# The prologue of a four-layer conditional kernel: batch weights from a small product, loads and first products in another order

## The chip, the cores and the metric

The kernel runs on one core of one Trainium2 chip. The metric is the device time of one execution in microseconds (us); lower is better. PE is TensorE, DVE is VectorE, ACT is ScalarE, POOL is GpSimd, SP is SyncE.

## The reference, cut to what matters

`x` has 16 batches of 128 rows by 128 channels, and `cond_8` has 8 weights for each batch. Four layers are added to `x` one after the other:

```
x = x + L0(x)   # the expert with the largest weight of the batch: silu gated MLP, 128 -> 256 -> 128, biases
x = x + L1(x)   # out = x W_base^T + b_base, and the low-rank part:
                #   h = einsum('btc,erc->bter', x, As)
                #   lora = einsum('bter,eor,be->bto', h, Bs, cond_8);  out + 2 * lora
x = x + L2(x)   # w_bot = einsum('bg,got->bot', cond_8, weight * mask);  x w_bot^T + bias
x = x + L3(x)   # softmax of cond_8, best two of 8 experts, gated gelu MLP 128 -> 512 -> 128,
                #   weighted sum, and one shared MLP of the same shape for all batches
```

## The kernel before

`x` is kept transposed in SBUF, channels on the partitions and 16 times 128 rows on the free axis. Every engine runs its own list of instructions, written out by hand, and the lists meet at semaphores. No planner moves anything: the order in the code is the order on the engine.

**The prologue (lines 257 to 526).** SP loads `cond_sb` (the weights and small tables, 16 partitions), `lora_sb` (the factors of L1) and `w2_sb` (the weights of L2). ACT's queue loads `cond_rep` (the batch weights, repeated on all 128 partitions by the DMA's access pattern), `small_sb` and all of `x`. While PE waits for inputs it multiplies constants into a bank that nobody reads (`warm`, line 487: five products of 512 columns, then some of 128). DVE finds the best experts of each batch (lines 684 to 689); a small product on PE (line 506) turns the expert numbers of the 16 batches into one row, DVE copies it to `at_row` (line 707), and SP reads it and starts the loads of the L0 experts into the ten slots of `ring0` (`load0`, lines 261 and 292 to 306). Two more small products (lines 509 and 510) count how often each expert was chosen; from these DVE and POOL sort the 32 pairs of batch and expert (lines 716 to 749 and 355 to 367), and the product of line 566, in the second step of the L0 loop, spreads the sorted list, `payload_sum`, over all partitions.

The prologue also makes one 128 by 128 matrix for each batch, for L1 and for L2. For L1, DVE scales the factor Bs by the batch weights (line 701, eight instructions for two batches each, into `bs_w`), and `prepare1` (line 492) multiplies by the factor As: eight products of 256 columns. For L2, `y_delta` (line 710) carries the batch weights, and 16 products of line 524 use 64 rows each. An f32 product stands as two records in the trace.

**L0 (lines 528 to 571).** For each batch `upgate0` makes four products of 128 columns (line 534), ACT applies silu, DVE multiplies, `down0` makes two products (line 542), and DVE adds to `x` (line 770).

**L1 and L2 (lines 550 and 576)** are 16 products each.

**L3 (lines 583 to 677)** goes through 48 units: 16 of the shared MLP ("S"), 24 of experts that are used by two batches each ("D") and 8 single ones ("R"). POOL splits the weights of S and D into a high and a low part first (lines 385 to 402), and PE makes three products for one.

Of the kernel before, what the change touches and what calls it, by code (L numbers as in the profile page):

```python
# [61 lines left out]
COND = SLOT + SLOTS  # L62
# [55 lines left out]
def build_kernel(nc, xT, cond, condT, lora, small, w2, experts0, experts3, shared, out):  # L118
    ctx = ExitStack()
    with ctx:  # L120
# [3 lines left out]
        def sem(name):  # L124
            return ctx.enter_context(nc.semaphore(name))
# [18 lines left out]
        cond_rep = sb("cond_rep", [P, B])  # L144
        ones = sb("ones", [B, P])
# [31 lines left out]
        payload_sum = sb("payload_sum", [B, 3, SLOTS])  # L177
# [20 lines left out]
        acc = [ctx.enter_context(nc.psum_tensor(f"acc{n}", [P, N], F32)) for n in range(2)]  # L198
        lin = pair[1] + pair[2]
# [4 lines left out]
        cond_in, rep_in, lora_in = sem("cond_in"), sem("rep_in"), sem("lora_in")  # L204
        small_in, w2_in = sem("small_in"), sem("w2_in")
        x_in, shared_in = sem("x_in"), sem("shared_in")
# [7 lines left out]
        ones_set, zeros_set = sem("ones_set"), sem("zeros_set")  # L214
# [41 lines left out]
        def _(sp):  # L256
            sp.dma_start(cond_sb[:, :], cond).then_inc(cond_in, 16)
            sp.dma_start(lora_sb[:, :], lora).then_inc(lora_in, 16)
# [35 lines left out]
            for b in range(4):  # L294
                load0(b)
            expert0 += values(mybir.EngineType.SP, at_row[0:1, 4:B], E)
# [3 lines left out]
            for b in range(SLOTS0, SLOTS0 + 2):  # L300
                load0(b)
# [3 lines left out]
            for b in range(SLOTS0 + 2, B):  # L305
                load0(b)
# [33 lines left out]
        def _(pool):  # L340
            pool.memset(ones_b[:, :], 1.0).then_inc(ones_set, 1)
            pool.memset(ones[:, :], 1.0).then_inc(ones_set, 1)
            pool.wait_ge(cond_in, 16)
# [22 lines left out]
            pool.tensor_tensor(payload_sum[:, :, :], payload[:, :, 0, :], payload[:, :, 1, :], ALU.add)\  # L366
# [38 lines left out]
        def _(act):  # L405
            rep = condT.unsqueeze(1).to_broadcast([2 * E, J, B])
            act.dma_start(cond_rep[:, :], rep).then_inc(rep_in, 16)
            act.dma_start(small_sb[:, :], small).then_inc(small_in, 16)
            act.dma_start(x[:, :], xT).then_inc(x_in, 16)
# [76 lines left out]
        def _(pe):  # L486
# [15 lines left out]
            warm(5)  # L502
# [4 lines left out]
            warm(2, P)  # L507
# [4 lines left out]
            warm(2, P)  # L512
            for q in range(G):
                prepare1(q)
# [13 lines left out]
            def upgate0(b):  # L528
                pe.wait_ge(e0_in[b % SLOTS0], 16 * (b // SLOTS0 + 1))
                if b >= FREE:  # L530
                    pe.wait_ge(hid0_done, (b - FREE + 1) * C0)
# [14 lines left out]
            pe.wait_ge(x_in, 16)  # L546
# [133 lines left out]
        def _(dve):  # L680
# [11 lines left out]
            dve.tensor_tensor(onehot[:, :, :], top_at[:, 0:K].unsqueeze(2).to_broadcast([B, K, E]),  # L692
# [245 lines left out]
```

## Time and profile before

| what | us |
|---|---|
| median of 3 runs | 150.93 (150.54 to 151.47) |
| the profiled execution | 151.12 |
| its span, first to last instruction | 149.2 |
| outside the span (151.12 less 149.2) | 1.9 |
| PE busy | 145.5 (98% of the span) |
| DVE busy | 108.3 (73%) |
| POOL busy | 93.5 (63%) |
| ACT busy | 71.5 (48%) |

The span is what the trace shows; the time of an execution is longer by what lies around it. Busy time of PE includes the products of constants.

### The profile page before, as it was taken

The numbers are of one execution on the slowest core, as the hardware profiler recorded it, in microseconds if no ns is written. First come the engines' busy times: TensorE is split into PE (matmuls) and PEld (weight loads), VectorE is DVE, ScalarE is ACT, GpSimd is POOL, SyncE is SP. The second block draws the span as 40 slices with busy tenths as digits, with TensorE's granted clock in tenths as the row PEclk, the third lists the DMA queues.
The fourth block names the chain that finished last, engine by engine and source line by source line (L and its number), as shares of the span: only waits on it lengthen the run. The fifth ranks groups of instructions, "written<-read, shape, count | busy, mean of one in ns | idle before, by whom it ended". The sixth has DMA issues, their size and how long they took to land.

```text
span 149.2 us, 3185 instructions
## 1 busy us (share of the span) xinstructions
PE 145.5 (98%) x1102; PEld 136.0 (91%) x1102; DVE 108.3 (73%) x226; ACT 71.5 (48%) x140; POOL 93.5 (63%) x109
## 2 busy tenths in 40 slices
PE   7999999999999999999999999999999999999992
PEld 3889999999978899999989999999999999999891
DVE  2935576668996577787876877877688896858792
ACT  3776445560465645454444535445445434346560
POOL 1169999999200395977977577968587999500000
PEclk9999999999999999999999999999999999999999
DMA  3999999986345675497195088637047606000052
GB/s 65 419 404 397 403 412 396 422 336 217 135 153 169 177 181 179 134 340 247 60 290 206 3 282 275 221 100 321 0 105 321 209 2 211 7 0 0 4 211 70
DMA packets 13919, 30.15 MB, mean 202 GB/s; under 512 B 1360, under 2 KB 8016, under 8 KB 13776
## 3 DMA queue, kind: packets, MB, share of 16 engines
q1 hardware_dynamic: 13472, 28.76, 54.6%
q10 hardware_dynamic: 432, 1.19, 2.3%
q8 instruction: 9, 0.15, 0.4%
q14 instruction: 6, 0.05, 0.1%
HBM read 24.70 MB, written 1.05 MB: 173 GB/s over the span
## 4 chain that ended last, share of the span: by engine, by line
PE 97%; DVE 1%; issue 0%
PE pair L603 23%; PE pair L593 15%; PE acc L652 11%; PE pair L534 10%; PE pair L610 10%; PE acc L637 7%; PE acc L542 5%; PE acc L661 5%; PE pair L498 2%; PE pair L579 2%; PE pair L554 2%; PE acc L489 2%; PE acc L524 1%; PE pair L524 1%; PE acc L498 1%; DVE lora_raw L843 1%
## 5 line engine op out<-in xcount | busy, mean ns | idle before, releaser
L810 DVE TENSOR_TENSOR hid_lo<-hid,hid_hi 128x512 fp32r<-128x512 f32 (+1 forms) x42 | 37.7, 898 | 17.0 <-ACT hid_hi L465 16.4
L400 POOL TENSOR_TENSOR duo_lo<-raw_duo,duo_hi 128x512 fp32r<-128x512 f32 x36 | 47.9, 1331 | 2.9
L465 ACT ACTIVATE hid_hi<-hid 128x512 fp32r<-128x512 f32 (+1 forms) x42 | 25.7, 611 | 43.4 <-DVE hid L817 39.2
L397 POOL CAST duo_hi<-raw_duo 128x512 fp32r<-128x512 f32 x36 | 27.5, 764 | 25.2 <-PE pair L603 19.3
L817 DVE TENSOR_TENSOR hid<-pair,act 128x512 f32<-128x512 f32 (+1 forms) x50 | 32.9, 662 | 4.6 <-PE pair L603 4.1
L603 PE MATMUL pair<-x_duo,duo_hi 128*128 128x256 f32 x192 | 35.2, 282 | 0.0
L450 ACT ACTIVATE act<-pair 128x512 f32<-128x512 f32 x47 | 27.6, 588 | 9.3 <-PE pair L603 7.0
L603 PEld LDWEIGHTS pair<-x_duo,duo_hi 128*128 128x128 f32 x192 | 29.7, 188 | 0.4
L603 PE MATMUL pair<-x_duo,duo_lo 128*128 128x256 f32 x96 | 27.0, 281 | 0.0
L593 PE MATMUL pair<-x_hl,shared_hi 128*128 128x512 f32 x64 | 20.5, 401 | 0.0
L603 PEld LDWEIGHTS pair<-x_duo,duo_lo 128*128 128x128 f32 x96 | 18.1, 189 | 0.0
L755 DVE SCALAR_TENSOR_TENSOR hid<-pair,ring,act 128x128 f32<-128x128 f32 x32 | 9.9, 347 | 9.9 <-PE pair L534 9.5
L534 PE MATMUL pair<-x,ring 128*128 128x128 f32 x128 | 16.9, 276 | 0.0
L534 PEld LDWEIGHTS pair<-x,ring 128*128 128x128 f32 x128 | 15.5, 192 | 0.1
L610 PE MATMUL pair<-x,raw_solo 128*128 x128 | 15.6, 275 | 0.0
L610 PEld LDWEIGHTS pair<-x,raw_solo 128*128 128x128 f32 x128 | 15.2, 192 | 0.3
L433 ACT ACTIVATE act<-pair,ring 128x128 f32<-128x128 f32 x32 | 10.0, 364 | 10.5 <-PE pair L534 10.5
L652 PE MATMUL acc<-hid_hi,duo_hi 128*128 128x256 f32 x48 | 14.1, 293 | 0.0
L652 PE MATMUL acc<-hid_lo,duo_hi 128*128 128x256 f32 x48 | 13.4, 279 | 0.0
L652 PE MATMUL acc<-hid_hi,duo_lo 128*128 128x256 f32 x48 | 13.4, 279 | 0.0
L593 PEld LDWEIGHTS pair<-x_hl,shared_hi 128*128 128x128 f32 x64 | 11.4, 188 | 2.1
L593 PE MATMUL pair<-x_hl,shared_lo 128*128 128x512 f32 x32 | 12.6, 395 | 0.0
(101 smaller groups left out, 202.6 us busy)
## 6 DMA issues: line engine op xcount, KB each, us to landing
raw_duo<-experts SPq DMA_DIRECT2D x12, 768.0 KB, 5.6
ring<-experts SPq DMA_DIRECT2D x16, 386.5 KB, 7.4
raw_solo<-experts SPq DMA_DIRECT2D x8, 768.0 KB, 4.3
x_duo<-x_hl SPq DMA_DIRECT2D x24, 128.0 KB, 3.3
x<-xT ACTq DMA_DIRECT2D x1, 1024.0 KB, 6.3
lora_raw<-x SPq DMA_DIRECT2D x4, 256.0 KB, 2.7
raw_solo<-shared SPq DMA_DIRECT2D x1, 768.0 KB, 10.9
out<-lora_raw SPq DMA_DIRECT2D x3, 256.0 KB, 2.6
```

The lines of the kernel that those rows point to most:

```text
L397: pool.tensor_copy(duo_hi[:, j % HALVES, piece(n)], raw_duo[:, j % RAWS, piece(n)])\
L400: pool.tensor_tensor(duo_lo[:, j % HALVES, piece(n)], raw_duo[:, j % RAWS, piece(n)], duo_hi[:, j % HALVES, piece(n)].bitcast(F32), ALU.su ...
L450: act.activation(act3[:, u % PAIRS, :], pair[u % PAIRS][0][:, :], ACT.Gelu_apprx_tanh)\
L465: act.activation(hid_hi[:, k % SPLITS, half(u, i)], hid3[:, u % PAIRS, half(u, i)], ACT.Copy)\
L534: ins = pe.matmul(pair[b % FREE][half][:, c * P:(c + 1) * P], ring0[:, b % SLOTS0, base + c * P:base + (c + 1) * P], x[:, cols(b)], start= ...
L593: ins = pe.matmul(bank[:, :].rearrange("p (b n) -> p b n", n=P), w[:, at], x_hl[:, n * GB:(n + 1) * GB, h, :], start=(m == 0), stop=(m == 2))
L603: ins = pe.matmul(bank[:, i * N2:(i + 1) * N2], w[:, n % HALVES, at], x_duo[:, n % GATHERS, h, :], start=(m == 0), stop=(m == 2))
L610: ins = pe.matmul(bank[:, m * P:(m + 1) * P], raw_solo[:, n % RAWS, base + m * P:base + (m + 1) * P], x[:, cols(solo_batch[n])], start=Tru ...
L637: ins = pe.matmul(y, w[:, at], v[:, k, half], start=(part == 0 and m == 0), stop=(part == C3 - 1 and m == 2), skip_group_check=True)
L652: ins = pe.matmul(y, w[:, n % HALVES, at], v[:, k, i * N2:(i + 1) * N2], start=(part == 0 and i == 0 and m == 0), stop=(part == 1 and i == ...
L810: dve.tensor_tensor(hid_lo[:, k % SPLITS, half(u, i)], hid3[:, u % PAIRS, half(u, i)], hid_hi[:, k % SPLITS, half(u, i)].bitcast(F32), ALU ...
L817: dve.tensor_tensor(hid3[:, u % PAIRS, half(u, i)], pair[u % PAIRS][1][:, half(u, i)], act3[:, u % PAIRS, half(u, i)], ALU.mult).then_inc( ...
```

## The change

Seven things are changed; the text of the other lines stays, with other line numbers.

1. `cond_rep` is no longer loaded. The table `cond` has 144 more columns: a 0/1 matrix that tells which weight each partition needs (`OF`), and the transposed weights (`TURNED`). A product of 8 rows and 16 columns writes `cond_rep` into the PSUM bank `pair[0][0]`, and DVE reads it there in all nine instructions that use it. The product stands after four, not five, products of 512 constant columns.
2. `lora_sb` is loaded first on ACT's queue, in the place of `cond_rep`, and no longer on SP's.
3. `x` is loaded in halves: the first on ACT's queue, the second on SP's, behind the first four expert loads. The second half gets a semaphore of its own, for which PE and DVE wait at batch 8.
4. `prepare1(0)`, two products of L1's preparation, stands ahead of the two products that count. Three products of 128 constant columns stand in front of it where two stood before the counting and two behind it.
5. On DVE the expert row's copy and the first scaling stand ahead of the comparison (`onehot`) and the sum (`chosen_b`) that the counting needs.
6. The product that spreads `payload_sum` has 128 rows, 112 of them zero, instead of 16. POOL writes the zeros at the start.
7. On SP, expert loads 12 and 13 stand ahead of the wait for the sorted list and of the first load for L3, not behind them.

```
--- before.py
+++ after.py
@@ -59,7 +59,8 @@
 
 
 EYE, IOTA, EARLIER, NUMBER, SLOT = E, E + B, 2 * E + B, 2 * E + 2 * B, 2 * E + 2 * B + 1
-COND = SLOT + SLOTS
+OF, TURNED = SLOT + SLOTS, SLOT + SLOTS + P
+COND = TURNED + B
...
-        cond_rep = sb("cond_rep", [P, B])
-        ones = sb("ones", [B, P])
+        ones = sb("ones", [P, P])
...
-        payload_sum = sb("payload_sum", [B, 3, SLOTS])
+        payload_sum = sb("payload_sum", [P, 3, SLOTS])
...
+        cond_rep = pair[0][0][:, 0:B]
...
         @block.sync
         def _(sp):
             sp.dma_start(cond_sb[:, :], cond).then_inc(cond_in, 16)
-            sp.dma_start(lora_sb[:, :], lora).then_inc(lora_in, 16)
             sp.dma_start(w2_sb[:, :, :], w2).then_inc(w2_in, 16)
 
             def load0(b):
@@ -293,16 +293,17 @@
             expert0 = list(values(mybir.EngineType.SP, at_row[0:1, 0:4], E))
             for b in range(4):
                 load0(b)
+            sp.dma_start(x[:, B // 2 * P:], xT[:, B // 2 * P:]).then_inc(x_in[1], 16)
             expert0 += values(mybir.EngineType.SP, at_row[0:1, 4:B], E)
             for b in range(4, SLOTS0):
                 load0(b)
             sp.dma_start(shared_sb, shared).then_inc(shared_in, 16)
-            for b in range(SLOTS0, SLOTS0 + 2):
+            for b in range(SLOTS0, B - 2):
                 load0(b)
             sp.wait_ge(slots_done, 1)
             duo_expert = values(mybir.EngineType.SP, slot_row[0:1, SLOTS:SLOTS + 2 * DUOS], E)
             load_duo(0)
-            for b in range(SLOTS0 + 2, B):
+            for b in range(B - 2, B):
                 load0(b)
             load_duo(1)
             solo_expert = values(mybir.EngineType.SP, slot_row[0:1, SLOTS + 2 * DUOS:2 * SLOTS], E)
...
@@ -340,6 +341,7 @@
         def _(pool):
             pool.memset(ones_b[:, :], 1.0).then_inc(ones_set, 1)
             pool.memset(ones[:, :], 1.0).then_inc(ones_set, 1)
+            pool.memset(payload_sum[:, :, :], 0.0).then_inc(sum_set, 1)
             pool.wait_ge(cond_in, 16)
             pool.tensor_copy(earlier_b[:, :], cond_sb[:, EARLIER:EARLIER + B]).then_inc(ones_set, 1)
...
             pool.wait_ge(placed_done, 3)
-            pool.tensor_tensor(payload_sum[:, :, :], payload[:, :, 0, :], payload[:, :, 1, :], ALU.add)\
+            pool.wait_ge(sum_set, 1)
+            pool.tensor_tensor(payload_sum[0:B, :, :], payload[:, :, 0, :], payload[:, :, 1, :], ALU.add)\
                 .then_inc(payload_done, 1)
...
         @block.scalar
         def _(act):
-            rep = condT.unsqueeze(1).to_broadcast([2 * E, J, B])
-            act.dma_start(cond_rep[:, :], rep).then_inc(rep_in, 16)
+            act.dma_start(lora_sb[:, :], lora).then_inc(lora_in, 16)
             act.dma_start(small_sb[:, :], small).then_inc(small_in, 16)
-            act.dma_start(x[:, :], xT).then_inc(x_in, 16)
+            act.dma_start(x[:, 0:B // 2 * P], xT[:, 0:B // 2 * P]).then_inc(x_in[0], 16)
...
-            warm(5)
+            warm(4)
+            pe.wait_ge(cond_in, 16)
+            pe.matmul(cond_rep[:, :], cond_sb[0:E, OF:OF + P], cond_sb[0:E, TURNED:TURNED + B], start=True, stop=True)\
+              .then_inc(rep_mm, 1)
             warm(4, P)
             pe.wait_ge(ones_set, 3)
             pe.wait_ge(at_diag_done, 1)
             pe.matmul(acc[1][:, 0:B], ones_b[:, :], at_diag[:, :], start=True, stop=True).then_inc(at_mm, 1)
-            warm(2, P)
+            warm(3, P)
+            prepare1(0)
             pe.wait_ge(chosen_done, 1)
             pe.matmul(pair[0][1][0:B, 0:E], earlier_b[:, :], chosen_b[:, :], start=True, stop=True)
             pe.matmul(pair[0][1][0:B, E:2 * E], ones_b[:, 0:B], chosen_b[:, :], start=True, stop=True)\
               .then_inc(rank_mm, 1)
-            warm(2, P)
-            for q in range(G):
+            for q in range(1, G):
                 prepare1(q)
...
             def upgate0(b):
                 pe.wait_ge(e0_in[b % SLOTS0], 16 * (b // SLOTS0 + 1))
+                if b == B // 2:
+                    pe.wait_ge(x_in[1], 16)
                 if b >= FREE:
                     pe.wait_ge(hid0_done, (b - FREE + 1) * C0)
...
-            pe.wait_ge(x_in, 16)
+            pe.wait_ge(x_in[0], 16)
...
             dve.tensor_tensor(at_diag[:, :], top_at[:, 0:1].to_broadcast([B, B]), cond_sb[:, EYE:EYE + B], ALU.mult)\
                .then_inc(at_diag_done, 1)
 
-            dve.tensor_tensor(onehot[:, :, :], top_at[:, 0:K].unsqueeze(2).to_broadcast([B, K, E]),
-                              cond_sb[:, IOTA:IOTA + E].unsqueeze(1).to_broadcast([B, K, E]), ALU.is_equal)\
-               .then_inc(onehot_done, 1)
-            dve.wait_ge(onehot_done, 1)
-            dve.tensor_tensor(chosen_b[:, :], onehot[:, 0, :], onehot[:, 1, :], ALU.add).then_inc(chosen_done, 1)
-            dve.wait_ge(rep_in, 16)
-            dve.wait_ge(lora_in, 16)
-            for i in range(2 * G):
+            def scaled_b(i):
                 at = slice(i * GB // 2, (i + 1) * GB // 2)
                 dve.scalar_tensor_tensor(
                     bs_w[:, at, :], lora_sb[:, BS1:BS1 + P].unsqueeze(1).to_broadcast([P, GB // 2, P]), LORA_SCALE,
                     cond_rep[:, at].unsqueeze(2).to_broadcast([P, GB // 2, P]), ALU.mult, ALU.mult)\
                    .then_inc(bsw_done, 1)
-                if i == 0:
-                    dve.wait_ge(at_mm, 1)
-                    dve.tensor_copy(at_row[:, :], acc[1][0:1, 0:B]).then_inc(at_done, 1)
+
+            dve.wait_ge(rep_mm, 1)
+            dve.wait_ge(lora_in, 16)
+            scaled_b(0)
+            dve.wait_ge(at_mm, 1)
+            dve.tensor_copy(at_row[:, :], acc[1][0:1, 0:B]).then_inc(at_done, 1)
+            dve.tensor_tensor(onehot[:, :, :], top_at[:, 0:K].unsqueeze(2).to_broadcast([B, K, E]),
+                              cond_sb[:, IOTA:IOTA + E].unsqueeze(1).to_broadcast([B, K, E]), ALU.is_equal)\
+               .then_inc(onehot_done, 1)
+            scaled_b(1)
+            dve.wait_ge(onehot_done, 1)
+            dve.tensor_tensor(chosen_b[:, :], onehot[:, 0, :], onehot[:, 1, :], ALU.add).then_inc(chosen_done, 1)
+            for i in range(2, 2 * G):
+                scaled_b(i)
 
             dve.wait_ge(small_in, 16)
             dve.tensor_tensor(y_delta[:, :, :], cond_rep[:, :].unsqueeze(2).to_broadcast([P, B, J]),
...
+                if b == B // 2:
+                    dve.wait_ge(x_in[1], 16)
...
+            np.tile(np.repeat(np.eye(E, dtype=np.float32), J, axis=1), (B // E, P // HALF)),
+            np.tile(arr(cond_8).T, (B // E, 1)),
         ]),
-        "condT": np.tile(arr(cond_8).T, (2, 1)),
```

On PE, from the products of constants to the first product of L2's preparation, before (acc, pair: PSUM banks; cond_sb, at_diag, chosen_b: the small tables):

```order
1 L489 MATMUL acc<-const-bfloat16-1.0 128x512 x5
2 L489 MATMUL acc<-const-bfloat16-1.0 128x128 x4
3 L506 MATMUL acc<-at_diag,ones_b 128x16
4 L489 MATMUL acc<-const-bfloat16-1.0 128x128 x2
5 L509 MATMUL pair_1<-chosen_b,earlier_b 16x8
6 L510 MATMUL pair_1<-chosen_b,ones_b 16x8
7 L489 MATMUL acc<-const-bfloat16-1.0 128x128 x2
8 L498 MATMUL pair_0<-bs_w,lora_sb 128x256 x2
9 L498 MATMUL pair_1<-bs_w,lora_sb 128x256 x2
```

and in the changed kernel:

```order
1 L491 MATMUL acc<-const-bfloat16-1.0 128x512 x4
2 L506 MATMUL pair_0<-cond_sb 128x16
3 L491 MATMUL acc<-const-bfloat16-1.0 128x128 x4
4 L511 MATMUL acc<-at_diag,ones_b 128x16
5 L491 MATMUL acc<-const-bfloat16-1.0 128x128 x3
6 L500 MATMUL pair_0<-bs_w,lora_sb 128x256 x2
7 L515 MATMUL pair_1<-chosen_b,earlier_b 16x8
8 L516 MATMUL pair_1<-chosen_b,ones_b 16x8
9 L500 MATMUL pair_1<-bs_w,lora_sb 128x256 x2
```

One product of 512 constant columns and one of 128 are gone, the product for `cond_rep` is new, and the counting has moved between the first two products of `prepare1` and the next ones.

On DVE in the same place, before:

```order
6 L689 TENSOR_TENSOR at_diag<-top_at,cond_sb 16x16 [waits route]
7 L692 TENSOR_TENSOR onehot<-top_at,cond_sb 16x16
8 L696 TENSOR_TENSOR chosen_b<-onehot 16x8 [waits onehot_done]
9 L701 SCALAR_TENSOR_TENSOR bs_w<-lora_sb,cond_rep 128x256 [waits lora_in,rep_in]
10 L707 CAST at_row<-acc 1x16 [waits at_mm]
11 L701 SCALAR_TENSOR_TENSOR bs_w<-lora_sb,cond_rep 128x256 x7
```

and in the changed kernel:

```order
6 L696 TENSOR_TENSOR at_diag<-top_at,cond_sb 16x16 [waits route]
7 L701 SCALAR_TENSOR_TENSOR bs_w<-lora_sb,pair_0 128x256 [waits lora_in,rep_mm]
8 L710 CAST at_row<-acc 1x16 [waits at_mm]
9 L711 TENSOR_TENSOR onehot<-top_at,cond_sb 16x16
10 L701 SCALAR_TENSOR_TENSOR bs_w<-lora_sb,pair_0 128x256
11 L716 TENSOR_TENSOR chosen_b<-onehot 16x8 [waits onehot_done]
12 L701 SCALAR_TENSOR_TENSOR bs_w<-lora_sb,pair_0 128x256 x6
```

The two instructions for the counting have moved behind the first scaling and around the second, and the scalings read `cond_rep` in PSUM (`pair_0`).

## Rows read from the trace of the kernel before

**Rows 1.** The page: busy time of the engines, and the chain's shares.

```profile
PE 145.5 (98%) x1102; PEld 136.0 (91%) x1102; DVE 108.3 (73%) x226; ACT 71.5 (48%) x140; POOL 93.5 (63%) x109
...
PE 97%; DVE 1%; issue 0%
```

**Rows 2.** The chain that ended last, pieces: start us, us, engine, tile, line, records.

```profile
0.79 2.72 PE acc L489 x9
3.51 0.12 PE acc L506
3.63 0.33 PE acc L489 x2
3.96 0.10 PE pair L509
...
4.41 2.72 PE pair L498 x8
...
8.00 0.86 PE pair L498 x4
...
10.84 1.98 PE pair L534 x16
...
13.27 0.89 PE pair L534 x8
14.16 0.39 PE pair L566 x2
14.55 0.64 PE acc L542 x4
...
16.09 0.45 PE acc L542 x4
```

**Rows 3.** Timeline of PE's weight loads: start us, us, then operation and idle before.

```profile
1.60 0.15 PEld L489 LDWEIGHTS acc<-const-bfloat16-1.0 128*128 128x128 bf16 x1 [0.28 <-issue]
2.03 0.15 PEld L489 LDWEIGHTS acc<-const-bfloat16-1.0 128*128 128x128 bf16 x1 [0.28 <-issue]
```

**Rows 4.** The instructions of line 498: ns min/median/max, first and last start.

```profile
L498 PEld LDWEIGHTS pair<-bs_w,lora_sb x12: 190/236/337, 4.1 to 8.3; 128*128 128x128 f32 x12
L498 PE MATMUL pair<-bs_w,lora_sb x12: 379/380/741, 4.2 to 8.5; 128*128 128x256 f32 x12
```

**Rows 5.** Timeline of DVE in the prologue.

```profile
2.55 0.16 DVE L684 MAX8 top<-cond_sb 16x8 f32<-16x8 f32 x1 [1.65 <-DMA cond_sb<-cond]
...
3.06 0.16 DVE L689 TENSOR_TENSOR at_diag<-top_at,cond_sb 16x16 bf16<-16x16 uint32 x1
...
3.60 0.43 DVE L701 SCALAR_TENSOR_TENSOR bs_w<-lora_sb,cond_rep 128x256 f32<-128x256 f32 x1
...
4.03 2.41 DVE L701 SCALAR_TENSOR_TENSOR bs_w<-lora_sb,cond_rep 128x256 f32<-128x256 f32 x7
6.37 0.27 DVE L710 TENSOR_TENSOR y_delta<-cond_rep,small_sb 128x128 f32<-128x128 f32 x1
```

**Rows 6.** Timeline: issues of two loads, and POOL's sum for the sorted list.

```profile
0.77 0.64 ACTq L407 DMA_DIRECT2D cond_rep<-condT  x1
...
1.22 0.41 SPq L258 DMA_DIRECT2D lora_sb<-lora  x1
...
9.88 0.37 POOL L366 TENSOR_TENSOR payload_sum<-payload 16x96 f32<-16x96 f32 x1
```

**Rows 7.** DMA issues up to 50 us: KB each, median us from issue to landing.

```profile
lora_sb<-lora SPq DMA_DIRECT2D x1, 128.0 KB, 2.3
cond_sb<-cond SPq DMA_DIRECT2D x1, 5.1 KB, 1.8
```

**Rows 8.** The page's groups: a DVE instruction that reads PSUM.

```profile
L755 DVE SCALAR_TENSOR_TENSOR hid<-pair,ring,act 128x128 f32<-128x128 f32 x32 | 9.9, 347 | 9.9 <-PE pair L534 9.5
```

**Rows 9.** Timeline of POOL: the split of L3's pair weights that it waited for.

```profile
50.97 0.61 POOL L397 CAST duo_hi<-raw_duo 128x512 fp32r<-128x512 f32 x1 [12.81 <-PE pair L603]
```

**Rows 10.** Windows, the L0 stage: us; busy of each engine; granted clock, DMA share, GB/s.

```profile
10.00:33.00 23.00, 23.00 (x211) 22.66 (x208) 13.94 (x49) 12.49 (x37) 22.68 (x30) 1.00 1.02 404
```

More of the change, by code:

```diff
@@ L115, with build_kernel @@
 SUMMED = dict(zip(ORDER, itertools.accumulate(additions(unit) for unit in ORDER)))
-def build_kernel(nc, xT, cond, condT, lora, small, w2, experts0, experts3, shared, out):
+def build_kernel(nc, xT, cond, lora, small, w2, experts0, experts3, shared, out):
     ctx = ExitStack()
@@ L202, in build_kernel @@
         mix = [[acc[1], pair[1][0]], [pair[1][1], pair[2][1]]]
-        cond_in, rep_in, lora_in = sem("cond_in"), sem("rep_in"), sem("lora_in")
+        cond_in, rep_mm, lora_in = sem("cond_in"), sem("rep_mm"), sem("lora_in")
         small_in, w2_in = sem("small_in"), sem("w2_in")
-        x_in, shared_in = sem("x_in"), sem("shared_in")
+        x_in, shared_in = [sem("x_in0"), sem("x_in1")], sem("shared_in")
         e0_in = [sem(f"e0_in{n}") for n in range(SLOTS0)]
@@ L213, in build_kernel @@
         route, weigh = sem("route"), sem("weigh")
-        ones_set, zeros_set = sem("ones_set"), sem("zeros_set")
+        ones_set, zeros_set, sum_set = sem("ones_set"), sem("zeros_set"), sem("sum_set")
         exp_done = sem("exp_done")
@@ L758, in hidden0 @@
                        .then_inc(hid0_done, 1)
-            dve.wait_ge(x_in, 16)
+            dve.wait_ge(x_in[0], 16)
             hidden0(0)
```

## The prediction

> **What bounds the kernel now.** I read the page's busy times and the chain of waits first. PE is busy for 145.5 of 149.2 us, and the chain that ended last is 97% PE [rows 1]. From 0.79 us on, each piece of the chain begins where the last one ended and is a piece of PE [rows 2]: PE never stands still, it works through its list in order. What remains of the span is the start (0.79 us) and the last store. So a load or a DVE result that comes earlier buys nothing by itself. The change can only gain by what it takes off PE's list, or by what its order saves PE between two products; and it can only lose by what it adds there, or by a wait that is longer than the work queued ahead of it.
>
> The second reading is how fast PE runs. The page's row of the granted clock has 9s in all slices, but the durations tell more. Two weight loads of the 512-column products start 0.43 us apart (1.60 and 2.03) [rows 3]: 512 columns in 0.43 us are 1.2 GHz, the lower level. In line 498 the records of one and the same form go from 741 down to 379 ns [rows 4], and the chain has eight of them in 2.72 us, but later four in 0.86 us, which is 0.215 each [rows 2]. At the lower level one takes twice 0.215, so 0.43. Of the eight, n with 0.43n + 0.215(8 - n) = 2.72 were slow: n is 4.6, and the clock rose at about 4.41 + 4.6 x 0.43 = 6.4 us. Ahead of that a product costs twice what it costs later.
>
> **The change part by part.** The sum is made against the profiled execution, 151.12 us, that is the span of 149.2 and 1.9 around it; it lies 0.19 above the median of 150.93.
>
> *One product of 512 constant columns less:* -0.43 us [rows 3].
>
> *The product for the batch weights:* new on PE, at the lower clock, after four long products, at 0.79 + 4 x 0.43 = 2.51 us. Nothing of this form is in the trace. From below: the bf16 product of 16 columns takes 0.12 in the chain (line 506) [rows 2]; this one is f32, two records, so 0.24. From above: the f32 product with few rows between products of 128 rows, line 566, takes 0.39, and the four records behind it 0.64 instead of 0.45, so it costs 0.39 + 0.19 = 0.58 at the higher clock [rows 2]; its weight loads, two of the 0.19 us that the slow form lengthens to 0.34 [rows 4], add 0.3 at the lower one: 0.9. I take 0.6, nearer to line 566, which has the same type and the same change of rows. There is also a wait: PE arrives at 2.51, and DVE could start on the table at 2.55 [rows 5], so 0.05 of the 0.6 is this wait. It grows if the table (144 more columns on 16 partitions) lands later; what is queued behind it is all of PE's list. Net with the first item: +0.17, between -0.2 and +0.5.
>
> *From line 506's product to the first product of `prepare1`:* before, 3.63 to 4.41 = 0.78 us, with four short constant products and the two that count [rows 2]. Two short constant products take 0.33 there, and 128 columns at 1.2 GHz are 0.11 of it each, so three take 0.44. That makes -0.34. Does the first scaling come in time for this? The weights' product ends at about 3.1, the LoRA tile is issued first on its queue; before it was issued at 1.22 [rows 6] and took 2.3 us [rows 7]; ACT's first issue was at 0.77 [rows 6], so it lands by 0.77 + 2.3 = 3.1. DVE is free after `at_diag` at 3.2 [rows 5]. So the first scaling starts at about 3.3 instead of 3.60, and ends at 3.7; PE wants it at about 4.2. No wait.
>
> *The counting, now between f32 products of 128 rows:* in the sum before it was part of the 0.78. Two bf16 products with 16 rows take 0.10 and 0.03 in the chain (the first is in the rows; the second is what lies between it and the next constant products) [rows 2]; line 566's manner, 0.58 less its two streams of 96 columns (0.08), gives 0.42. I take 0.35, near line 566: +0.35, between 0.13 and 0.42.
>
> *DVE's list:* DVE now waits for PE's new product, and behind that wait stand the scalings and the expert row's copy, on which SP's expert loads wait. The scalings read PSUM. An instruction with 128 columns and a PSUM operand takes 347 ns [rows 8], the `y_delta` one from SBUF 273 [rows 5]: +0.07 each at most. Seven scalings came in 2.41 us, 0.34 each, now 0.41 [rows 5]. PE takes one in two records, 0.86 at the lower clock and 0.43 at the higher: it stays the slower of the two. The last scaling ends at 3.3 + 8 x 0.41 + 0.4 for the three small ones between = 7.0; PE wants it at about 8.2 and `y_delta` at 8.9. The counting's chain on DVE and POOL moves by some 0.6 us; its sum ended at 9.88 + 0.37 = 10.25, and PE takes it at 14.16 [rows 2, 6]. This slack of 3.9 us hides it, as it hides POOL's added memset.
>
> *The product of 128 rows instead of 16 (line 566):* 16 rows cost 0.58 as worked out above. With 128 rows it would be two records among their like, eight of which take 0.89, so 0.22 [rows 2]. That is -0.36. The same penalty of a change of rows shows where line 524's 64-row products end: the 16 records that follow take 1.98, and twice 0.89 would be 1.78 [rows 2].
>
> Against this stands a rule: the Trainium skill, TensorE: Matmul & The Clock Gate, section LDWEIGHTS (loading the stationary operand), says that a load with 32 rows takes as long as one with 128, since only the columns count. By that rule this part would be worth 0, and the whole sum +0.18 instead of -0.18. The row of the weight loads agrees for the load itself; what the chain shows is the gap around it.
>
> *Loads:* `x` is first read by PE at 10.84, and the chain shows no wait there [rows 2], so all of it had landed; the first half lands no later, and the second has until batch 8, seven steps of 0.89 + 0.45 after the first one. The expert row, for which SP waits with the expert loads, moves with its product, by 0.17 at most; they too have until 10.84. Loads 12 and 13 stand ahead of the first pair's load for L3, and they are half its size each; at 404 GB/s, with the DMA engines full [rows 10], their 0.77 MB put 1.9 us ahead of it. POOL, which splits these weights for PE, stood still for 12.81 us until 50.97, because PE had not yet used the last split [rows 9]. A delay of 1.9 us disappears in that; without this cover it would be the cost. I put it at nothing.
>
> **Sum:** -0.43 + 0.60 - 0.34 + 0.35 - 0.36 = -0.18. From 151.12 that gives 150.9, and from the median of 150.93 gives 150.7. Adding the ends: lowest -0.43 + 0.24 - 0.34 + 0.13 - 0.36 = -0.76; highest -0.43 + 0.9 - 0.34 + 0.42 + 0 = +0.55.
>
> **The rivals.** *First, the row count is not what makes line 566 dear.* Its bank or its neighbour could be. For it: the rule above. Against it: the same 0.2 behind the 64-row products. Time: 150.93 + 0.18 = 151.1. Chance 0.12.
>
> *Second, the wait for the table holds PE.* The new product is the first in the list to wait for a load. The table's rows are nearly three times as long, and the LoRA tile, 128 KB, is issued at the same moment on the other queue instead of 0.45 later. If the table lands 0.5 late, everything behind moves by 0.5. For it: DVE shows that it landed only at 2.5, just where PE arrives. Against: both are small. Time: 150.7 + 0.5 = 151.2. Chance 0.15.
>
> *Third, slower: the clock rises later.* The stretch before the rise now has a wait and three changes of rows in it, where PE does no columns; before, it was nearly unbroken. If for that reason it rose only behind `prepare1`, the eleven records that were fast would take 0.43 instead of 0.215 each: +2.4 us, 153.1. Each us that the rise comes later costs half a us of work, so from 3 us on it would be 1%. Against: PE's list has nearly the same length up to there, and idle added by the wait and the changes of rows is a few tenths. Chance 0.06.
>
> *Fourth, faster by over 1%.* All constant products together are 2.72 + 0.66 us of PE's list, and the change drops only two of them; the rest of the head is needed work. I see no mechanism for 1.5 us. Chance 0.02 for under 149.4.
>
> **How the numbers follow.** The forecast, a change of -0.18, has 0.65; its own range from the bounds and the spread of the runs (150.54 to 151.47) is 150.1 to 151.4. The first two rivals lie at 151.1 and 151.2 and want 151.6 with the same spread. So 150.1 to 151.6 leaves out the clock case and the tails. One per cent, 1.5 us, is about what a measurement of this kernel can tell from no change: faster than 149.4 0.02, slower than 152.4 0.06, the rest 0.92 within 1%.
>
> **What the profile of the changed kernel would show.** The new product starts at 2.5 to 2.6 and ends by 3.2. The first scaling starts at about 3.3. `prepare1` starts at about 4.2 in the chain, 0.17 ahead of 4.41 and not more, since PE's list ahead of it has hardly become shorter; the counting after it takes 0.3 to 0.4. Line 573, the spreading, takes 0.22 and the four records behind it 0.45. PE's share stays at 97%. Wrong would be: a PE idle time ahead of the new product of over 0.2; slow records of line 500 beyond the fifth; or `prepare1` waiting for DVE. The time would be off if the clock's rise lay elsewhere, which it may also do from run to run.

## The result and the profile after

The changed kernel takes 152.0 us (median of 8 runs, 151.62 to 152.69), the kernel before 150.72 in the same call (8 runs, 150.2 to 151.47). The ratio is 1.0082, with a 95% interval of 1.0061 to 1.0103: slower by 0.8%. The forecast was 150.7, its range ended at 151.6. A ratio below goes by all undisturbed runs of its call, so it can differ from the quotient of the two medians beside it, by up to 0.4%.

The page of the changed kernel: its span, then each engine's busy time, share and instructions.

```profile
span 149.8 us, 3187 instructions
...
PE 145.9 (97%) x1102; PEld 136.2 (91%) x1102; DVE 105.9 (71%) x226; ACT 72.0 (48%) x140; POOL 93.9 (63%) x110
```

PE is busy as before [rows 1]; the profiled run took 151.74 us. Which stretch is longer shows in the chain of the changed kernel, the piece's start, its length, and what it is:

```profile
0.75 2.02 DMA cond_sb<-cond
2.77 0.04 issue
2.81 0.60 PE pair L506 x2
3.42 0.54 PE acc L491 x4
3.96 0.12 PE acc L511
4.08 0.43 PE acc L491 x3
4.51 1.81 PE pair L500 x4
6.32 0.10 PE pair L515
6.42 0.03 PE pair L516
6.45 1.58 PE pair L500 x4
8.03 0.86 PE acc L500 x4
8.89 0.86 PE pair L500 x4
9.76 0.30 PE acc L529
...
11.74 1.98 PE pair L541 x16
...
15.07 0.20 PE pair L573 x2
15.26 0.47 PE acc L549 x4
```

The chain now begins with a load: PE waits for the table. L1's preparation starts at 4.51 where it started at 4.41, and its last piece ends at 9.76, before at 8.00 + 0.86 = 8.86 [rows 2]. That is +0.90. At the first product that reads `x` it is still +0.90 (11.74 against 10.84). The 128-row product and the four behind it give back (0.39 + 0.64) - (0.20 + 0.47) = 0.36. So +0.54 of the +0.62 between the two profiled runs (151.74 - 151.12) lies in the first 16 us. Behind that PE lies late by the same half microsecond to the end (its first product of L3 starts at 40.51, before at 39.96): nothing later costs it anything in this run. Nearly all of the loss is in `prepare1`: its first eight records take 1.81 + 1.58 = 3.39 us, before 2.72.

How many of them ran at the lower clock? By the prediction's way of counting such a record takes 0.43, and one at the higher clock 0.215. The first four, all at the lower clock, took 0.09 more (1.81 - 4 x 0.43). The second four stand behind the counting. Two experiments below show what it takes in front of them. In a_both all four ran at the lower clock and took 0.29 more than 4 x 0.43; in a_warm6 all four ran at the higher one and took 0.20 more than 4 x 0.215:

```profile
6.38 2.01 PE pair L500 x4
```
```profile
6.15 1.06 PE pair L500 x4
```

So the second four of the changed kernel held (1.58 - 0.29 - 0.86) / 0.215 = 2.0 records at the lower clock, six with the first four. The clock rose at about 6.45 + 0.29 + 2.0 x 0.43 = 7.6 us. Before, with the same 0.09, there were (2.72 - 0.09 - 1.72) / 0.215 = 4.2 such records and the rise was at 4.41 + 0.09 + 4.2 x 0.43 = 6.3; the prediction's 4.6 and 6.4 left the 0.09 out. The rises below are estimated in this way. The records of line 500 show the same two levels (count, then shortest, median and longest in ns):

```profile
L500 PE MATMUL pair<-bs_w,lora_sb x12: 379/528/796, 4.3 to 9.4; 128*128 128x256 f32 x12
```

The median is 528 here and was 380 [rows 4]: more of them ran at the lower clock. If the clock rises at r and all work before it runs at half speed, a run takes W + r/2, where W is what it would take at 2.4 GHz throughout. Before: 151.12 - 6.3 / 2 = 148.0. After: 151.74 - 7.6 / 2 = 147.9. On this reading W did not change and the rise explains the difference; by the medians r would be 5.4 and 8.2 (estimates from that formula). The pieces say the same. With the rise left at 6.3, `prepare1` would hold 4.0 records at the lower clock and 12.0 at the higher, and end at about 4.51 + 0.09 + 4.0 x 0.43 + 12.0 x 0.215 + 0.33 = 9.2, where the 0.33 is the counting (0.13 and the 0.20). That is some 0.36 late, just what the 128-row product gives back. The other 0.54 is the later rise. In these terms a piece of the low-clock stretch costs only half its length, which the sum of the prediction did not allow for.

The loads changed too. Windows of one us at 6 to 7 us (busy share of PE, PEld, DVE, ACT, POOL, then granted clock, DMA share, GB/s), of before and of after, and SP's issues of after:

```profile
6.00:7.00 1.00, 1.00 (x6) 0.88 (x5) 0.98 (x7) 0.60 (x1) 0.09 (x1) 1.00 1.03 434
```
```profile
6.00:7.00 1.00, 1.00 (x5) 0.63 (x5) 1.00 (x6) 0.60 (x1) 0.00 (x0) 1.00 0.72 189
```
```profile
5.00 2.02 SPq L265 DMA_DIRECT2D ring<-experts  x4
7.07 0.42 SPq L296 DMA_DIRECT2D x<-xT  x1
8.45 3.31 SPq L265 DMA_DIRECT2D ring<-experts  x6
11.81 0.50 SPq L300 DMA_DIRECT2D raw_solo<-shared  x1
```

The DMA engines moved 189 GB/s in that microsecond instead of 434. The second half of `x` isn't issued before 7.07, behind expert loads that need the experts' numbers; until then less is queued. The shared expert's load is issued at 11.81 (before 10.64). In this run PE doesn't wait for any of it. Note that the clock column shows 1.00 in both rows, at 6 us, while the products still take 0.43: in the prologue it doesn't show the lower level, the durations do.

### The profile page after: what moved, and what is told of

Its sections match the earlier page's. It is cut to its first block, busy times and chain, and to the rows that moved or that the text cites. A ratio compares the mean times of both kernels' runs of the same rounds, so it can differ in the third digit from the quotient of the medians.

```text
span 149.8 us, 3187 instructions
## 1 busy us (share of the span) xinstructions
PE 145.9 (97%) x1102; PEld 136.2 (91%) x1102; DVE 105.9 (71%) x226; ACT 72.0 (48%) x140; POOL 93.9 (63%) x110
## 4 chain that ended last, share of the span: by engine, by line
PE 96%; DMA 1%; DVE 1%; issue 0%
PE pair L610 23%; PE pair L600 15%; PE acc L659 11%; PE pair L541 10%; PE pair L617 10%; PE acc L644 7%; PE acc L668 5%; PE acc L549 5%; PE pair L500 3%; PE pair L586 2%; PE pair L561 2%; DMA cond_sb<-cond 1%; PE acc L529 1%; PE acc L491 1%; PE pair L529 1%; PE acc L500 1%
## 5 line engine op out<-in xcount | busy, mean ns | idle before, releaser
L403 POOL TENSOR_TENSOR duo_lo<-raw_duo,duo_hi 128x512 fp32r<-128x512 f32 x36 | 48.9, 1359 | 2.9
L823 DVE TENSOR_TENSOR hid_lo<-hid,hid_hi 128x512 fp32r<-128x512 f32 (+1 forms) x42 | 34.8, 829 | 16.0 <-ACT hid_hi L467 15.3
L400 POOL CAST duo_hi<-raw_duo 128x512 fp32r<-128x512 f32 x36 | 26.7, 742 | 25.8 <-PE pair L610 18.6
```

The lines of the kernel that those rows point to most:

```text
L400: pool.tensor_copy(duo_hi[:, j % HALVES, piece(n)], raw_duo[:, j % RAWS, piece(n)])\
L403: pool.tensor_tensor(duo_lo[:, j % HALVES, piece(n)], raw_duo[:, j % RAWS, piece(n)], duo_hi[:, j % HALVES, piece(n)].bitcast(F32), ALU.su ...
L823: dve.tensor_tensor(hid_lo[:, k % SPLITS, half(u, i)], hid3[:, u % PAIRS, half(u, i)], hid_hi[:, k % SPLITS, half(u, i)].bitcast(F32), ALU ...
```

## The experiments

Theory C: the clock's rise comes later, and that is the loss. Theory W: PE's wait for the table. Theory L: the later loads. No kernel changes the outputs; one adds a product whose result is unused. "b" kernels start from before, "a" kernels from after. Diffs are cut.

**Cover the wait** with one and two more long products. Label a_warm6, and a_warm5 with `warm(5)`:

```
-            warm(4)
+            warm(6)
             pe.wait_ge(cond_in, 16)
```

> The changed kernel with six instead of four products of 512 constant columns ahead of the product for the batch weights: PE works until about 0.8 + 6 x 0.43 = 3.35 us and no longer stands still for the table, which landed at 2.8 in the changed kernel. Theory C (the standstill of about 0.2 to 0.4 us ahead of the new product makes the clock rise later, 7.4 us instead of 6.2 in the two profiles, and that is most of the loss): the slow records of line 500 end earlier again, on average as in the kernel before; two more products at the lower clock cost 0.86 less the 0.37 of standstill covered, 0.5 us of low-clock time, or 0.25 us; in all 0.6 to 1.0 us faster than the changed kernel, about 151.1 to 151.4. Theory W (the new product and the counting between f32 products cost their own time, the clock's rise is chance): the two added products only add, 152.0 + 0.25 = 152.2 or more.

> The changed kernel with five instead of four products of 512 constant columns, and nothing else. Theory C+L: the clock rises earlier as in the one before, but PE then meets the late loads and the x_hl instruction that POOL holds, as with six products: 151.6 to 152.3, a narrow spread. If the clock alone matters: 150.8 to 151.2.

a_warm6: 152.61 us, ratio 1.0122 (1.0097 to 1.0147). a_warm5: 152.62, 1.012 (1.009 to 1.015). The wait is gone in both and nothing is gained, so theory W falls. In a_warm5 the rise is at about 8.4 (the first four take 1.81, the second four 1.87, so 3.3 of these were slow), W is 152.1 - 4.2 = 147.9: it pays by the clock. a_warm6 is another case. Its chain has `prepare1` all fast (four in 1.09), and it isn't faster. Its rise came ahead of `prepare1`, at about 4.5. Its waits (engine, line, who it waited for, us, times, longest), and the DVE and the POOL instruction behind them:

```profile
PE pair L600 <- DVE x_hl L796: 0.7, 1, 0.7
PE pair L541 <- DMA ring<-experts: 0.2, 1, 0.2
```
```profile
39.65 1.61 DVE L796 TENSOR_TENSOR x_hl<-x,x_hl 128x512 fp32r<-128x512 f32 x1
```
```profile
39.44 1.27 POOL L403 TENSOR_TENSOR duo_lo<-raw_duo,duo_hi 128x512 fp32r<-128x512 f32 x1
```

In the changed kernel the same DVE instruction begins at 39.67 and takes 0.68; POOL's last subtraction had begun at 38.50 there. Here it begins at 39.44 and ends at 40.71, and DVE's instruction ends 0.55 after that (41.26), 0.9 late, as though it had stood until POOL was done. Lined up with before's, PE's pieces lose 0.35 us at 24 us and 0.45 at 30, each time at an expert load, and 0.9 at this instruction. So the loads are a second floor, hidden in the profiled run of the changed kernel behind a late PE.

**The standstill alone** (b_gap), in before:

```
-            warm(5)
+            warm(3)
+            pe.wait_ge(cond_in, 16)
+            warm(2)
```

> The kernel before, with nothing changed but a wait for the table put behind the third of the five products of 512 constant columns, so that PE stands still from about 2.1 to 2.6 us and no work is added. Theory C: the clock rises later as in the changed kernel, by one to two us or more, and each us costs half a us; with half of the 0.5 us of idle itself 0.9 to 1.3 us slower than before, about 151.7 to 152.1. Theory W: only the idle counts, 0.25 to 0.5 us, 151.0 to 151.3.

151.66 us against 150.6, ratio 1.0068 (1.0038 to 1.0098), and wide: 150.79 to 152.74. Its chain:

```profile
0.76 1.52 DMA cond_sb<-cond
2.28 0.05 issue
2.33 1.46 PE acc L489 x6
...
4.69 2.62 PE pair L498 x8
```

PE stands still for a quarter of a us (0.79 + 3 x 0.43 = 2.08 to 2.33). `prepare1` starts 0.28 later than before, at half price 0.14; the median lost 1.06. The profiled run, one of the short ones, doesn't show where the others lost it (rise at 6.4, W 148.1). A variable rise would do that, and it is argued, not seen.

**The small product alone** (b_small), its result unused, behind five long products, where its inputs are there:

```
             warm(5)
+            pe.wait_ge(cond_in, 16)
+            pe.wait_ge(ones_set, 2)
+            pe.matmul(pair[0][0][:, 0:B], ones[0:E, :], cond_sb[0:E, EYE:EYE + B], start=True, stop=True)
```

> The kernel before with one small f32 product (8 rows, 128 by 16 columns) added behind the five products of 512 constant columns; its result goes to a bank where nobody reads it, and the batch weights are loaded as before. PE does not stand still, since the table lands at 2.5 and PE comes at 2.9. Theory P (a product with so few columns ahead of the rise makes the clock rise later, as a standstill does): the rise comes one to two us later in most runs, with 0.3 us for the 0.6 us of low-clock work 0.8 to 1.3 us slower than before, 151.6 to 152.2. If only a standstill does that: +0.3, 151.1.

152.9 us against 150.75, ratio 1.0128 (1.009 to 1.0165). It adds 0.53 in the chain and costs 2.15:

```profile
0.79 2.29 PE acc L489 x5
3.08 0.53 PE pair L505 x2
...
5.06 3.52 PE pair L498 x8
8.58 1.01 PE acc L498 x4
9.59 0.86 PE pair L498 x4
```

All eight are slow and most of one more: rise at about 8.9, W 148.35. This is theory C by itself: no load and no order is changed, PE doesn't wait for the inputs (its pieces touch), and the rise comes 2.6 us later. Nor is it the chance of one profile: the six runs (152.03 to 153.5) lie wholly above before's 23 (150.2 to 151.42).

**Loads and their order.** Part 3 alone on before (b_halves), part 7 alone on before (b_new_order), and from after, `x`'s second half back on ACT's queue (a_x_act), the order of part 7 undone (a_old_order), both (a_both):

```
+            act.dma_start(x[:, B // 2 * P:], xT[:, B // 2 * P:]).then_inc(x_in[1], 16)      # a_x_act, a_both
-            for b in range(SLOTS0, B - 2):
+            for b in range(SLOTS0, SLOTS0 + 2):                                             # a_old_order, a_both
```

> The kernel before with x in halves, the second behind the first four expert loads (part 3 alone). Theory P: the DMA engines run dry at 6 to 7 us and all later loads land 0.8 us later; that shows only where PE comes early: 150.7 to 151.2, the lowest runs up from 150.3 by some tenths. If the dry stretch is a main cause: 151.3 or more.

> The kernel before with part 7 alone: expert loads 12 and 13 ahead of the wait for the sorted list. Theory L: the first pair's load lands at 27.4 instead of 25.4, POOL's sixth split ends at 38.9 to 40 instead of 38.2, which meets DVE's x_hl (39.1 in the profile before, earlier in faster runs): 0 to 0.7 us slower, 150.8 to 151.4, and the lowest time rises from 150.2. Theory W: no change, 150.7.

> The changed kernel with both halves of x on ACT's queue, the second right behind the first, as early as all of x was before. Theory L (loads: in the changed kernel the DMA engines run dry at 6 to 7 us, 189 GB/s where there were 434, because half of x now comes behind four expert loads; all later loads land some 0.9 to 2.8 us later, POOL's split of the first pairs ends later, and DVE's x_hl instruction, which doesn't finish while POOL's subtraction runs, holds PE in the runs in which PE comes early): the loads land 0.7 to 0.9 us earlier than in the changed kernel, 0.5 to 0.9 us faster, 151.1 to 151.5. Theory W (the new product and the counting's new place cost PE their own time and push the clock): no change, 152.0.

> The changed kernel with the expert loads 12 and 13 back behind the wait for the sorted list and the first load for L3's pairs (part 7 undone). Theory L: the first pair lands 1.9 us earlier, POOL's sixth split ends before DVE's x_hl starts, and the floor that this sets is gone; what is left is the dry stretch, which may hold PE at expert load 12: 0.5 to 1.0 us faster, 151.0 to 151.5. Theory W: no change, 152.0.

> The changed kernel with both undone: x on ACT's queue in two halves one behind the other, and the old order of loads 12 and 13. Theory L: all of the loss is in these two, 150.6 to 150.9, the time of the kernel before less what the 128-row product brings. Theory W: no change, 152.0.

b_halves 151.49 against 150.75, 1.0046 (1.0027 to 1.0064). b_new_order 150.73 against 150.72, 0.9998. a_old_order 152.37, 1.0104 (1.0072 to 1.0136). a_x_act 152.93, 1.0159. a_both 152.72, 1.0121. In b_halves PE waits for a load, at a rise (5.6) that is no later than before's:

```profile
PE pair L537 <- DMA ring<-experts: 0.4, 1, 0.4
```
```profile
6.00:7.00 1.00, 1.00 (x6) 0.90 (x5) 1.00 (x7) 0.73 (x2) 0.03 (x1) 1.00 1.08 320
```

So the halves cost 0.74 by themselves, the order nothing. In the changed kernel undoing part 7 gains nothing either, and the profiled run has lost nothing behind 16 us; as the main cause of that run's loss theory L falls. Part 3 has no clean test there: a_x_act and a_both bring something new, late in L3:

```profile
PE acc L659 <- DVE hid_lo L823: 0.6, 1, 0.6
```
```profile
52.94 1.56 DVE L823 TENSOR_TENSOR hid_lo<-hid,hid_hi 128x512 fp32r<-128x512 f32 x1 [0.76 <-ACT hid_hi L467]
```
```profile
51.96 0.61 POOL L399 CAST duo_hi<-raw_duo 128x512 fp32r<-128x512 f32 x1 [13.54 <-PE pair L610]
52.65 1.29 POOL L402 TENSOR_TENSOR duo_lo<-raw_duo,duo_hi 128x512 fp32r<-128x512 f32 x1
```

Again a DVE instruction that takes 0.68 elsewhere is held while POOL subtracts. W of a_both is 153.44 - 4.3 = 149.1, some 1.2 above after's. Lined up with before's, PE's pieces lose 1.5 us behind 16 us in a_both, and 1.1 in the other kernels of this kind. ACT's `hid_hi` had come 0.3 late (idle ahead of it 1.25, in after 0.94). That turns the order of the two instructions round. In after DVE's begins first, by 0.04; it keeps its 0.69, and POOL's takes 1.81 instead of 1.3:

```profile
52.15 0.69 DVE L823 TENSOR_TENSOR hid_lo<-hid,hid_hi 128x512 fp32r<-128x512 f32 x1 [0.76 <-ACT hid_hi L467]
52.19 1.81 POOL L403 TENSOR_TENSOR duo_lo<-raw_duo,duo_hi 128x512 fp32r<-128x512 f32 x1
```

In these records the one that begins first keeps its time, and only DVE's delay reaches PE. Every kernel here with four DMAs on ACT's queue had the late `hid_hi` and the wait at line 659, none with three; why ACT comes late is open. Less 1.1 to 1.5, a_both would be at 151.2 to 151.6, under the changed kernel's 152.0: a share of the loads is not excluded.

**Both cures together** (a_both with `warm(5)`, and with `warm(6)`):

> The kernel in which x is loaded on ACT's queue and loads 12 and 13 stand in their old place, with one more change: five, not four, products of 512 constant columns ahead of the product for the batch weights, so that PE works until 2.87 us and does not stand still for the table, which lands at 2.7. Theory C+L (the standstill makes the clock rise later, and only where it rises early do the late loads hold PE): the slow records of line 500 end before 6.5 us in most runs, the loads are on time, 150.5 to 151.0. If only the standstill and the clock matter, the same. If the new product itself, 0.5 us with few columns, keeps the clock down: no faster than the kernel without the fifth product, 152.4 or more.

> The changed kernel with the loads' old places (x on ACT's queue in two halves, loads 12 and 13 behind the sorted list) and six products of 512 constant columns ahead of the product for the batch weights. If the clock and the loads are all of it: in the runs in which the clock rises before 5 us the loads are late by the 0.5 us only by which the expert row is later, and the time is 151.0 to 151.6; runs with a later rise lie up to 153. If something else in the change costs 1 us: no run under 152.2.

153.58, 1.0144, and 153.63, 1.0145 (1.0099 to 1.0192). The clock rose at about 9.9 and 9.3 in the profiles; both carry the wait at line 659. With six long products ahead of the small one the rise was at 4.5 in a_warm6 and at 9.3 here, with the same list on PE up to there: it differs from run to run by microseconds. Two of six runs of both_warm6 took 151.95 and 152.13. Less 1.1 that is near before's time, but no profile shows such a run.

**Parts 4 and 5** alone on before (b_count), and undone in after (a_count_early); parts 3 to 7 without 1 and 2 (b_parts37):

```
-            warm(2, P)
+            warm(3, P)
+            prepare1(0)
...
-            warm(2, P)
-            for q in range(G):
+            for q in range(1, G):
```

> The kernel before with the counting between the first products of prepare1 and the next ones, and DVE's list in the new order (parts 4 and 5 alone). Theory P: PE's list changes by under 0.1 us and the stretch ahead of prepare1 becomes denser, so no change or a little faster: 150.5 to 150.9. If the change of rows between f32 products at the lower clock costs by itself: 151.1.

> The changed kernel with the counting back ahead of all products of prepare1, between the short constant products, on PE and on DVE (parts 4 and 5 of the change undone, the rest kept). Theory C: the standstill stays, so the clock stays late; the counting's place is worth under 0.2 us: 151.8 to 152.1. Theory W: the counting's 0.26 us between the f32 products and what follows it are a third of the loss: 151.6.

> Parts 3 to 7 of the change on the kernel before; the batch weights and the LoRA tile are loaded in their old places, and five products of 512 constant columns stand at the start (parts 1 and 2 undone). Theory P: the table's product and wait are what cost, so this has 150.4 to 151.0. If the loads' order and the counting cost much: 151.5 or more.

b_count 151.08 against 150.75, 1.0013 (0.9995 to 1.0032): nothing gained, since PE waits 0.2 for DVE's first scaling. a_count_early 152.48, 1.0121: undoing them doesn't help either. Its rise is at 7.3, still late without the counting in its new place, and PE waits 0.3 for the same DVE instruction as in a_warm6. b_parts37 152.39, 1.0097 (1.0066 to 1.0128), with a rise by 6.2 at the latest (its second four take 1.06): here the loss is the loads'. The same two instructions as in a_warm6 meet:

```profile
39.48 1.59 DVE L793 TENSOR_TENSOR x_hl<-x,x_hl 128x512 fp32r<-128x512 f32 x1
```
```profile
39.26 1.27 POOL L403 TENSOR_TENSOR duo_lo<-raw_duo,duo_hi 128x512 fp32r<-128x512 f32 x1
```

**Part 1 undone in after** (a_rep_load: `cond_rep` loaded again, no product, `warm(5)`), and the LoRA tile on ACT's queue behind `cond_rep` in b_rows_12 below (b_rows_lora):

```
+            act.dma_start(cond_rep[:, :], condT.unsqueeze(1).to_broadcast([2 * E, J, B])).then_inc(rep_mm, 16)
...
-            pe.matmul(cond_rep[:, :], cond_sb[0:E, OF:OF + P], cond_sb[0:E, TURNED:TURNED + B], start=True, stop=True)\
```

> The changed kernel with the batch weights loaded again (second on ACT's queue, behind the LoRA tile), no product for them and five products of 512 constant columns: part 1 undone, parts 2 to 7 kept. Theory C+L: no standstill, the clock rises as in the kernel before; what the loads cost remains: 151.0 to 151.6. If the loads' new order costs nothing: 150.4 to 150.7.

> The kernel before with the 128-row product, load 12 ahead of the wait for the sorted list, and the LoRA tile behind cond_rep on ACT's queue, so that SP issues the weights of L2 0.45 us earlier into the stretch in which the DMA engines moved only 172 GB/s. If loads hold PE in the fast runs, these come 0.2 us earlier: 150.2 to 150.4. If they don't any more: 150.4, as with load 12 alone. If the LoRA tile lands after 4.2 us, PE waits for the first scaling and it is slower, 150.9 or more.

154.89, 1.0265, and 154.35, 1.0248. Neither tests its part cleanly. With the two loads one behind the other on ACT's queue the second landed at 5.2 to 5.4, and PE stood still:

```profile
PE pair L500 <- DVE bs_w L698: 1.6, 1, 1.6
```

Their chains reach the first product that reads `x` at 13.36 and 13.50, 2.5 and 2.7 us behind before's 10.84, for a wait of 1.6: the rise came at about 9.4 and 9.8. The four DMAs on ACT's queue and the wait at line 659 add 1.1 in each.

**Part 6** alone on before (b_rows128), and with load 12 issued ahead of the first pair (b_rows_12):

```
+        payload_sum = sb("payload_sum", [P, 3, SLOTS])
...
-            for b in range(SLOTS0, SLOTS0 + 2):
+            for b in range(SLOTS0, SLOTS0 + 3):      # b_rows_12
```

> The kernel before with only the product that spreads the sorted list made with 128 rows, 112 of them zero. Both theories: 0.36 us faster (150.4), since in the changed kernel's profile this product took 0.20 with 0.47 for the four records behind it, where it had taken 0.39 and 0.64. The rule that rows don't matter: 150.8, no change.

> The kernel before with the product of 128 rows and expert load 12 alone ahead of the wait for the sorted list. In the kernel with the 128-row product PE waited some 0.2 us for load 12 in the run with the early clock. Both theories: that wait goes, the first pair lands 1 us later, which POOL's idle time and the 0.9 us before x_hl just hide: 150.2 to 150.5, the lowest of all.

b_rows128: 150.46 against 150.6, 0.9989 (0.9972 to 1.0005). b_rows_12: 150.41 against 150.9, **0.9968 (0.9948 to 0.9988)**, the only version faster than before. Its chain has the gain in full, and in b_rows128's, 0.25 of it goes to one group of eight (1.14 instead of 0.89), which load 12 held; it is gone in b_rows_12:

```profile
4.41 2.28 PE pair L500 x8
6.69 0.86 PE acc L500 x4
...
13.72 0.20 PE pair L568 x2
13.92 0.47 PE acc L544 x4
```
```profile
26.19 1.14 PE pair L536 x8
```

## Why the prediction was wrong

**The step that failed**: the sum left the clock's rise where it was, and gave its moving no term. It stood only as the third rival, "the clock rises later", which got 0.06. That rival's mechanism is what happened, between its case and none: the rise at 7.6 instead of 6.3 in the profile, not behind all of `prepare1`. The sign that the prediction named for it, slow records of line 500 beyond the fifth, came: there were six. Its "against" was the error: "idle added by the wait and the changes of rows is a few tenths". So it was, and a few tenths are enough. b_gap lost 1.06 us by one standstill, b_small 2.15 by 0.53 us of a product with few columns.

The profiles part by that product. With it behind four or five long ones the rise lies at 7.2 to 9.9 (after, a_old_order, a_count_early, a_x_act, a_both, a_warm5, both_warm5, b_small). Without it, and without the long wait of a_rep_load and b_rows_lora, it lies at 4.7 to 6.4 (before, b_new_order, b_rows128, b_rows_12, b_halves, b_count, b_parts37, b_gap). Behind six long ones it was at 4.5 once and at 9.3 once.

The rival's price, "half a us" for each us of rise, held: W stays between 147.6 and 148.4 in before, after, b_new_order, b_rows128, b_rows_12, b_gap, b_small, a_old_order, a_warm5, b_count and a_count_early, while r goes from 4.7 to 8.9. In the others W is higher, and each shows PE waiting for a load or for a DVE result.

Of the terms of the sum:

- The product for the batch weights with its wait, 0.60, was mis-sized: measured 0.89. Where it doesn't wait it takes 0.53 (a_warm5), and the four short products behind it take 0.54 instead of 0.43: 0.64. Its wait, put at 0.05, was 0.25: it ended at 3.42, where a_warm5's end less one long product, 0.78 + 2.29 + 0.53 - 0.43, is 3.17. The table's load took 2.02 from issue to landing instead of 1.8 [rows 7]. The second rival, this wait as the cause, is refuted by a_warm5.
- From line 506's product to `prepare1`, 0.44: measured 4.51 - 4.08 = 0.43. `prepare1` at 4.2: 4.51, by the 0.29 that the product and its wait took more. The first scaling at 3.3: 3.46, and PE didn't wait for it.
- The counting, 0.35: 0.13 in the chain, and 0.29 more in the four behind it at the lower clock: 0.42, the upper end of its range.
- The 128-row product, -0.36: measured -0.36. Here row and rule stood against each other. By the Trainium skill, TensorE: Matmul & The Clock Gate, section LDWEIGHTS (loading the stationary operand), the time of a load doesn't depend on its row count. The load itself nearly agrees (181 to 184 ns with 16 rows, 192 with 128), but the chain gives back 0.36 when 16 rows become 128, in after, b_rows128 and b_rows_12. The first rival is refuted.
- All terms at the lower clock, -0.43, +0.60, -0.34 and +0.35, counted whole, where they cost half. That alone would have made the forecast -0.27 instead of -0.18: a small error.
- "Loads: I put it at nothing." Wrong as a statement on the edits: the halves cost 0.74 alone (b_halves). The cover that I named, POOL's 12.81 us of idle [rows 9], is still 11.72 us long in after, but it lies behind the place that is hit: the pairs' weights land later, POOL's last split before that idle ends later, and a DVE instruction in PE's path is held by it (a_warm6, b_parts37). In the profiled run of after it just misses: 38.50 + 1.28 = 39.78 against 39.67. How often it hits in the other runs isn't shown.

What stays open: what part of the 1.28 us between the medians is the loads'. The profiled runs differ by 0.62 and place it in the first 16 us; for the rest the rise would have to lie at about 8.2 in the median run, and at 5.4 in before's, which no profile of these two caught. Nor does any run separate the wait from the product within the changed kernel; covering the wait alone did not bring the rise back. Why the product delays the rise is open too.

## What to carry to other kernels

In a prologue that runs at the lower clock, the gaps matter more than the lengths: a short product or a standstill of a few tenths may delay the rise by microseconds, so put small products behind the rise, or take their result from a load. Read the rise from the durations in the chain, and compare versions by time less half the rise: what is left of the difference is the work. Before calling a later load free, follow it to each engine that shares the path, not only to the one whose idle time is long.

## What the runs showed of the hardware

- A constant two-record f32 product with 16 columns, between bf16 products of 512 and of 128 columns, moved the rise from about 6.3 to 8.9 us (b_small).
- A DVE instruction with its operands in SBUF (128x512, 0.68 us) took 1.54 to 1.61 where a POOL subtraction of 128x512 had begun 0.2 to 0.3 us ahead of it. Where the DVE instruction began 0.04 ahead, it kept its time and the subtraction took 1.81 instead of 1.3 (after, at 52.15). The held one ended 0.54 to 0.56 us after the subtraction in a_warm6, b_parts37 and a_both, and 0.55 in a_count_early (1.24 long). In after, where only 0.11 of the subtraction was left, the same DVE instruction kept its 0.68 and ended 0.57 behind it. The two DVE instructions ahead of it in after, which read PSUM, took 1.57 together (0.74 is one alone), nearly all of it beside the same subtraction: they weren't held.
- 16 rows instead of 128 cost 0.36 us around one f32 product of two records, with 181 to 184 against 192 ns for the load (before, after).
- Four DMAs on ACT's queue at the start went together with an ACT instruction 0.3 us later at 50 us, and 1.1 to 1.5 us in all, in six kernels of six. Only the coincidence is shown.
